# Which engine multiplies which scan state: eight transposed states in every scan order

## The chip, the cores and the metric

The kernel runs on one core of a Trainium2 chip. The metric is the device time of one execution in microseconds; all numbers are float32. Five engines work in it, each with its own queue that it follows in order: TensorE (PE: matmuls, transposes), VectorE (DVE: scans, products), ScalarE (ACT: activations, PSUM copies), GpSimd (POOL: products in SBUF) and SyncE (SP: the DMAs). They wait for each other with semaphores.

## The reference, cut to what matters

Eight images of 192 x 48 x 48 go through two layers. The first is a state-space layer: group norm, a projection to 384 channels, a 3x3 depthwise convolution and gelu give `u`, which is scanned in four orders (`k`: by rows, by columns, and both backwards).

```python
xs = jnp.stack([x_hw, x_wh, x_hw[..., ::-1], x_wh[..., ::-1]], axis=1)
def step(h, xs_t):                          # 2304 positions, 16 states for each of 384 channels
    d_t, u_t, B_t, C_t = xs_t
    dA = jnp.exp(d_t[..., None] * A)
    h = h * dA + (d_t * u_t)[..., None] * B_t[:, :, None, :]
    y = jnp.einsum('bkdn,bkn->bkd', h, C_t)  # sum over the 16 states
    return (h, y)
ys = ys[:, 0:2] + ys[:, 2:4, :, ::-1]
y = ys[:, 0] + ys[:, 1].reshape(Bb, Dd, Ww, Hh).transpose(0, 1, 3, 2).reshape(Bb, Dd, L)
```

`delta` (`d_t`) is the softplus of a small projection of `u`. After the scan come a layer norm over channels, a gate and an output projection; the second layer is an attention. The change touches the scan alone.

## The kernel before

**Chunks, orders, states.** One image's scan runs through four orders `k` of six chunks `c` of 384 positions each (24 chunks, numbered `q`), with 16 states `i` a chunk and three groups `j` of 128 channels a state. The loop over the eight images is a loop on the chip; the chunks are written out.

**What a state costs each engine.** ScalarE makes `dA` as exp into PSUM bank 2 + j (L1554), when the scan of the state before has read that bank. GpSimd makes delta times u times B for all three groups in one product (`delta_u_b`, L1794), three states ahead of the scan. VectorE scans (L1229), three instructions a state, into one of `NH = 4` state buffers `hb`. The last column of each state is saved by ScalarE as the start of the next chunk (`hold_state`, L1498, semaphore `carry`), because the product with C overwrites the buffer. Then the state is multiplied by its row of C and summed over the states into PSUM banks 5 to 7 (y), in one of three ways, which `Plan` fixes:

- *pool*: GpSimd multiplies by a broadcast row of C (`times_c`, L1804), after the scan and after `hold_state` of that state, and TensorE adds the result with an identity matmul (`state_sum`, L756, six passes).
- *dve*: ScalarE copies the row of C to PSUM bank 1 (`c_copy`, L1514), VectorE multiplies (`times_c`, L1257), and TensorE adds as above.
- *turn*: TensorE transposes the state in three tiles of 128 positions into PSUM bank 0 (`turn`, L734); ScalarE multiplies each tile by a column of C, as its per-partition scale, into one of three buffers `ht` (`turned_product`, L1523); TensorE transposes it back with a matmul that adds to y (`turned_sum`, L743). Bank 0 holds one tile, so the next can be turned only when ScalarE has read the last.

**The order on the queues.** TensorE goes through slots m = 0 to 15 of a chunk (slots 16 and 17 lie in the next chunk). In slot m it does delta's matmul (m = 1, 4, 7, for the next chunk), a *unit* if there is one, and then `slot(q, m)`: the sums that are due, and the tiles n + 1 + t = m of the turned states n, one or two. A dve state is summed in slot n + 2, a pool state in n + 3. In slots 5, 8 and 11 it adds a third of the y of the earlier orders (`y_chunk`, L820; L817 in order 0). ScalarE goes through steps i: for each j an exp, and after the second and third the products of the tiles of slot i - 1; then `hold_state(i - 1)`, a unit's copy (`unit_out`), the softplus's ln, `c_copy(i - 1)`, in steps 2 and 3 the stores of the last chunk's y (`store_y`, L1542), and the other softplus steps (abs, exp) of the next chunk's delta. VectorE does the scans of state i, then the product with C of state i - 1 if it is a dve state, and in steps 5, 8 and 11 delta (L1178). GpSimd does `delta_u_b(i + 3)`, then `times_c(i)` if i is a pool state, and after state 12 the next chunk's delta times u (L1779).

**PSUM bank 1** serves in turn delta's matmuls, the ln of the softplus, the rows of C, and the *units*: in orders 0 to 2 each chunk makes two 128-channel pieces of the next image's input projection (L787), whose copies (L1531, L1534) DMAs take away.

**The plans.** Orders 0 and 1 have four pool states (0, 3, 6, 9), five turned (1, 4, 7, 10, 13) and seven dve; orders 2 and 3 have three (0, 6, 9), seven (1, 3, 4, 7, 10, 12, 13) and six (2, 5, 8, 11, 14, 15). In the latter the slots 4 to 6 and 13 to 15 have two tiles.

**y by columns.** y lies in SBUF by rows. In orders 1 and 3 a chunk is eight columns; its 384 values are read and stored with a stride of 48 in SBUF, in the sequence in which PSUM holds them.

Of the kernel before, what the change touches and what calls it, by code (L numbers as in the profile page):

```python
# [97 lines left out]
LAST = PLANS[-1]  # L98

# [17 lines left out]
def made_s(b, q, n):  # L117
    return b * S_ALL + (LAST.ns + S_TO[q] + n)
# [36 lines left out]
UK = 3  # L155
# [9 lines left out]
def build(nc, t, out):  # L165
    ctx = ExitStack()
    with ctx:
# [465 lines left out]
        def _(e):  # L633
# [87 lines left out]
            def scan_phase(b, x_proj, turn_c):  # L721
# [43 lines left out]
                def slot(q, m):  # L765

                    p = plan(q)
                    for i in p.order:
                        if p.sum_at[i] == m and i in p.pool:
                            state_sum(q, i)  # L770
                    for at in p.slots[m][:1]:
                        tile(q, at)
                    if m == N + 1:
                        turned_sum(q, p.nt - 1)
                    for i in p.order:
                        if p.sum_at[i] == m and i in p.dve:
# [12 lines left out]

                def body(k, c, par, last, nxt):  # L790
                    g = e.snap(b * 24 + (c + k * NC))
                    q = k * NC + c
                    h = e.snap(b * UC + (c + k * NC)) if k < UK else None
                    for m in range(N):
# [7 lines left out]
                        if k < UK and m in plan(q).units:  # L802
                            unit(k, h, q, plan(q).units.index(m))
# [10 lines left out]
                        if m in ADD_AT:  # L814
                            j = ADD_AT[m]
                            if k == 0:
                                e.matmul(ps[:, 5 + j, 0:CH], d_diag[:, j], u_v[:, 0, j, ds(pos(k, c), CH)],  # L817
                                         start=False, stop=False)
                            else:
                                e.matmul(y_psum(k)[:, j], ident[:], y_chunk(k, c)[:, j], start=False, stop=False)  # L820
# [596 lines left out]
        def _(e):  # L1417
# [76 lines left out]
            def scan_phase(b):  # L1494
                def hold_state(k, c, i):
# [4 lines left out]
                def c_copy(g, q0, i, nxt, h=None):  # L1500
# [7 lines left out]
                    if nxt and i in (5, 8, 11):  # L1508
                        e.wait_ge(dp_v, g * 3 + (3 + (i - 2) // 3))
# [3 lines left out]
                    e.wait_ge(hcs, made_d(b, q0, d))  # L1513
                    e.activation(ps[:, 1, 0:CH], row_c[:, q % 2, i % ROWS], ACT.Copy).then_inc(c_ps, 1)  # L1514

                def turned_product(k, c, at):
# [4 lines left out]
                    e.wait_ge(turn_mm, made_t(b, q, at + 1))  # L1521
                    e.wait_ge(turn_sum, made_t(b, q, at - 2))
# [13 lines left out]
                def store_y(g, k, c, j, final=False):  # L1536
# [4 lines left out]
                    e.wait_ge(turn_sum, made_t(b, k * NC + c, plan(k * NC + c).nt))  # L1541
                    e.activation(y_chunk(k, c)[:, j], y_psum(k)[:, j], ACT.Copy).then_inc(yev, 1)  # L1542

                def body(k, c, par, last, nxt):
                    g = e.snap(b * 24 + (c + k * NC))
                    g16, g48, q = e.snap(g * 16), e.snap(g * 48), k * NC + c
                    h = e.snap(b * UC + (c + k * NC)) if k < UK else None
                    e.wait_ge(dp_v, g * 3 + 3)
                    for i in range(N):
# [378 lines left out]
```

## Time and profile before

| | |
|---|---|
| median of 3 runs | 14,696.73 us (14,694.96 to 14,697.96) |
| the profiled execution | 14,691.09 us, span 14,689.3 us |
| busy: TensorE, VectorE, ScalarE, GpSimd | 90%, 88%, 76%, 70% |
| granted TensorE clock | 0.991 |

The span is what lies between the first and the last instruction of the profiled execution. Busy shares are means over the scan and the other stages; the work of the scan repeats in 24 chunks an image and 192 in all, so 0.1 us a chunk is 19 us of the time.

### The profile page before, as it was taken

How to read it: one execution, taken by the hardware profiler on the slowest of the kernel's cores; microseconds unless marked ns; L12 is line 12 of the kernel's file. 1: busy time of each engine (PE TensorE's matmuls, PEld its weight loads, DVE VectorE, ACT ScalarE, POOL GpSimd, SP SyncE). 2: the span in 40 equal slices, each digit the busy share in tenths (PEclk: the TensorE clock that was granted, in tenths of full speed). 3: DMA queues.
4: the chain of work that ended last, by engine and by line, in shares of the span. 5: the costliest groups of instructions: out<-in, count | busy, mean ns of one | idle time of the engine just before them, and what ended most of it. 6: DMA issues, size and time to landing. Idle time of an engine off the chain costs nothing.

```text
span 14689.3 us, 247142 instructions
## 1 busy us (share of the span) xinstructions
PE 13181.2 (90%) x65256; PEld 8153.8 (56%) x65256; DVE 12970.4 (88%) x13833; ACT 11123.1 (76%) x22914; POOL 10326.6 (70%) x4126
## 2 busy tenths in 40 slices
PE   6888988889888998889988899888998889988899
PEld 4566455664556645566455664556645566455654
DVE  8999689996899978999689996899969999599995
ACT  5888578885788857887578876788767887678875
POOL 6999069980699807998079970899708996099960
PEclk9999999999999999999999999999999999999999
DMA  3443023430343303443033430344303442043420
GB/s 114 129 131 124 25 93 128 130 124 21 97 130 129 119 21 102 130 141 103 21 111 128 140 96 21 116 130 138 91 21 123 131 138 83 21 131 128 138 78 26
DMA packets 907982, 1468.60 MB, mean 100 GB/s; under 512 B 38912, under 2 KB 891904, under 8 KB 893664
## 3 DMA queue, kind: packets, MB, share of 16 engines
q1 hardware_dynamic: 906560, 1452.37, 31.2%
q8 instruction: 559, 9.16, 0.3%
q14 instruction: 863, 7.07, 0.1%
HBM read 1350.07 MB, written 102.17 MB: 99 GB/s over the span
## 4 chain that ended last, share of the span: by engine, by line
PE 33%; issue 24%; POOL 16%; DVE 15%; ACT 7%; DMA 2%; DVEq 1%; ACTq 1%; POOLq 0%; SPq 0%
POOL area L1794 12%; DVE area L1229 9%; PE ps L756 7%; PE ps L1030 5%; PE ps L1042 5%; DVE area L1257 4%; PE ps L743 3%; POOL area L1804 3%; PE ps L734 3%; ACT ps L1554 3%; DMA area<-bc_rows 2%; PE ps L892 2%; ACT area L1523 2%; PE ps L724 2%; PE ps L856 1%
## 5 line engine op out<-in xcount | busy, mean ns | idle before, releaser
L1229 DVE TENSOR_TENSOR_SCAN area<-ps,hst,area 128x384 f32<-128x384 f32 x9216 | 8581.8, 994 | 150.5 <-ACT ps L1554 69.6
L1794 POOL TENSOR_TENSOR area<-area 128x1152 f32<-128x1152 f32 x3072 | 7998.3, 2638 | 62.6 <-POOL area L1779 29.4
L1554 ACT ACTIVATE ps<-area,a_neg 128x384 f32<-128x384 f32 x9216 | 5259.7, 580 | 984.8 <-DVE area L1229 959.2
L756 PE MATMUL ps<-area,ident 128*128 128x384 f32 x11472 | 4127.3, 494 | 441.5 <-POOL area L1804 408.2
L756 PEld LDWEIGHTS ps<-area,ident 128*128 128x128 f32 x11472 | 2050.0, 191 | 1918.6 <-POOL area L1804 449.4
L743 PE MATMUL ps<-ident,area 128*128 128x128 f32 x20736 | 2882.2, 275 | 0.0
L743 PEld LDWEIGHTS ps<-ident,area 128*128 128x128 f32 x20736 | 2604.0, 192 | 50.3 <-ACT area L1523 1.5
L1523 ACT ACTIVATE area<-ps,area 128x384 f32<-128x384 f32 x3456 | 1972.6, 571 | 560.2 <-PE ps L734 559.4
L1714 ACT ACTIVATE area<-ps,t_neg,area 128x768 f32<-128x768 f32 x1728 | 1617.8, 986 | 1001.1 <-PE ps L1030 1001.1
L1774 POOL TENSOR_TENSOR area<-area,ones 128x2304 f32<-128x2304 f32 x16 | 85.2, 5352 | 3103.5 <-ACT area L1483 2980.9
L734 PE MATMUL ps<-ident,area 128*128 128x128 f32 x10368 | 1765.2, 279 | 326.4 <-ACT area L1523 314.0
L734 PEld LDWEIGHTS ps<-ident,area 128*128 128x128 f32 x10368 | 1260.7, 141 | 1334.1 <-ACT area L1523 568.9
L1804 POOL TENSOR_TENSOR area<-area 128x1152 f32<-128x1152 f32 x672 | 1771.5, 2636 | 153.0 <-DVE area L1229 123.5
L1257 DVE TENSOR_TENSOR area<-area,ps 128x1152 f32<-128x1152 f32 x1248 | 1658.7, 1329 | 17.0 <-ACT ps L1514 17.0
L1030 PE MATMUL ps<-area 64*128 64x384 f32 x6912 | 1374.7, 517 | 28.4 <-ACT area L1645 11.5
L1042 PE MATMUL ps<-area 128*64 128x384 f32 x6912 | 1322.8, 501 | 0.0
L1030 PEld LDWEIGHTS ps<-area 64*128 64x128 f32 x6912 | 604.2, 189 | 766.5 <-ACT area L1714 493.1
L1042 PEld LDWEIGHTS ps<-area 128*64 128x64 f32 x6912 | 441.7, 137 | 780.0 <-issue 776.9
L724 PE MATMUL ps<-area,w_dt 128*128 128x384 f32 (+1 forms) x1104 | 489.4, 525 | 360.7 <-DVE area L1257 356.7
L416 DVE SCALAR_TENSOR_TENSOR area<-area,w_dw 128x1152 f32<-128x1152 f32 (+1 forms) x640 | 802.7, 1329 | 0.0
L1514 ACT ACTIVATE ps<-area 128x384 f32<-128x384 f32 x1248 | 609.8, 489 | 93.7 <-DMA area<-bc_rows 70.2
L787 PE MATMUL ps<-xz,w_in 96*128 96x384 f32 x1152 | 445.5, 509 | 161.1 <-DVE area L1257 161.0
(163 smaller groups left out, 9539.6 us busy)
## 6 DMA issues: line engine op xcount, KB each, us to landing
area<-bc_rows SPq DMA_DIRECT2D x1536, 768.0 KB, 6.7
xz<-x_normed SPq DMA_DIRECT2D x144, 288.0 KB, 6.3
area<-in_x SPq DMA_DIRECT2D x18, 1728.0 KB, 10.1
area<-x_padded SPq DMA_DIRECT2D x24, 1250.0 KB, 12.1
z_raw<-z_st SPq DMA_DIRECT2D x144, 192.0 KB, 6.2
area<-z_raw SPq DMA_DIRECT2D x8, 3456.0 KB, 14.9
x_padded<-x_st SPq DMA_DIRECT2D x120, 200.0 KB, 7.8
x_normed<-area SPq DMA_DIRECT2D x9, 1728.0 KB, 8.1
```

What stands on the lines that cost most here:

```text
L734: i = e.matmul(ps[:, 0, j * 128:(j + 1) * 128], hb[:, n % NH, j, tt * 128:(tt + 1) * 128], ident[:], is_transpose=True)
L743: i = e.matmul(ps[:, 5 + j, tt * 128:(tt + 1) * 128], ht[:, at % 3, j * 128:(j + 1) * 128], ident[:], start=False, stop=False)
L756: m = e.matmul(ps[:, 5 + j, 0:CH], ident[:], hb[:, i % NH, j], start=i == 0, stop=i == N - 1)
L1030: i = e.matmul(ps[:, 2 * ((2 * m + h) % 3) + s, 0:CH], kz[rows, p, m * 128:(m + 1) * 128], q_v[rows, p, c * QC + s * CH:c * QC + (s + 1) * ...
L1042: i = e.matmul(ps[64 * h:64 * h + 64, 6 + s, 0:CH], vt[:, p, m, 64 * h:64 * h + 64], pb[:, w % 4, s * CH:(s + 1) * CH], start=m == 0, stop ...
L1229: e.tensor_tensor_scan(rev(hb[:, i % NH, j], k), rev(ps[:, 2 + j, 0:CH], k), rev(dbu[:, i % NH, j], k), hst[:, i, j:j + 1], ALU.mult, ALU. ...
L1257: e.tensor_tensor(hb[:, i % NH], hb[:, i % NH], ps[:, 1:2, 0:CH].broadcast_to([128, J, CH]), ALU.mult).then_inc(hcs, 1)
L1523: e.activation(ht[:, at % 3], ps[:, 0, 0:CH], ACT.Copy, scale=c_t[:, ds(t + (k % 2 * MT + tt), 1), k // 2 * N + n]).then_inc(turn_cp, 1)
L1554: e.activation(ps[:, 2 + j, 0:CH], dlt[:, par, j], ACT.Exp, scale=a_neg[:, j, k, i:i + 1]).then_inc(da, 1)
L1714: e.activation(pb[:, w % 4].rearrange("p (s l) -> p s l", s=2), ps[:, 2 * (w % 3):2 * (w % 3) + 2, 0:CH], ACT.Exp, scale=ksc[:, p, w:w + 1 ...
L1794: e.tensor_tensor(dbu[:, i % NH], du[:, par], row_b[:, q % 2, i % ROWS:i % ROWS + 1].broadcast_to([128, J, CH]), ALU.mult).then_inc(dbus, 1)
L1804: e.tensor_tensor(hb[:, i % NH], hb[:, i % NH], row_c[:, q % 2, i % ROWS:i % ROWS + 1].broadcast_to([128, J, CH]), ALU.mult).then_inc(hcp, 1)
```

## The change

All four orders get one plan: pool states 0, 9, 11; turned states 1, 3, 4, 6, 7, 10, 12, 13; dve states 2, 5, 8, 14, 15. Two tiles now lie in slots 4 to 9 and 13 to 15. State 11 is summed in slot 13. The units move to slots 12 and 14; the second one, and the adds of y, go ahead of the slot's second tile, and the sums of a slot with two tiles, those of pool states too, stand between the tiles. Bank 1's waits follow (`after_ln`, `ln_free`, unit 0 after the last delta, unit 1 after unit 0's copy). In orders 1 and 3 y is read and stored in runs of eight values in SBUF, and it is the PSUM side that goes with a stride of 48. Some sums of semaphore counts are worked out once a chunk.

```diff
 class Plan:
-    def __init__(self, pool, turn, units):
+    def __init__(self, pool, turn, units, early={}):
...
-        self.sum_at = {n: n + 3 for n in pool} | {n: n + 2 for n in self.dve}
+        self.sum_at = {n: n + 3 for n in pool} | {n: n + 2 for n in self.dve} | early
...
+        self.late = units[0] > 11
+        self.ln_free = max(n for n in self.dve if n < 10)
+        self.after_ln = {5: 1, 8: 2, min(n for n in self.dve if n > 10): 3}
...
-FIVE = Plan((0, 3, 6, 9), (1, 4, 7, 10, 13), (10, 14))
-SEVEN = Plan((0, 6, 9), (1, 3, 4, 7, 10, 12, 13), (10, 13))
-PLANS = (FIVE, FIVE, SEVEN, SEVEN)
+EIGHT = Plan((0, 9, 11), (1, 3, 4, 6, 7, 10, 12, 13), (12, 14), {11: 13})
+PLANS = (EIGHT,) * K
...
-            return y_v.rearrange("p j (h w) -> p j w h", h=H)[:, :, ds(c * 8 if k < 2 else (NC - 1) * 8 - c * 8, 8), :]
+            return y_v.rearrange("p j (h w) -> p j h w", h=H)[:, :, :, ds(c * 8 if k < 2 else (NC - 1) * 8 - c * 8, 8)]
...
-            return p if k % 2 == 0 else p.rearrange("p j (w h) -> p j w h", w=8)
+            return p if k % 2 == 0 else p.rearrange("p j (w h) -> p j h w", w=8)
...
-                def slot(q, m):
+                def slot(q, m, between=None):
 
                     p = plan(q)
-                    for i in p.order:
-                        if p.sum_at[i] == m and i in p.pool:
-                            state_sum(q, i)
+                    sums = [i for i in p.order if p.sum_at[i] == m]
+                    if len(p.slots[m]) < 2:
+                        for i in sums:
+                            if i in p.pool:
+                                state_sum(q, i)
                     for at in p.slots[m][:1]:
                         tile(q, at)
                     if m == N + 1:
                         turned_sum(q, p.nt - 1)
-                    for i in p.order:
-                        if p.sum_at[i] == m and i in p.dve:
+                    for i in sums:
+                        if i in p.dve or len(p.slots[m]) == 2:
                             state_sum(q, i)
+                    if between:
+                        between()
                     for at in p.slots[m][1:]:
                         tile(q, at)
...
                 def unit(k, h, q, i):
...
+                    if i == 1:
+                        e.wait_ge(unit_ev, h * 2 + 1)
+                    elif plan(q).late:
+                        e.wait_ge(dp_v, b * 72 + (3 * q + 6))
...
+                def filler(k, c, h, q, m):
+                    add_y(k, c, m)
+                    if k < UK and m == 14 and plan(q).late:
+                        unit(k, h, q, plan(q).units.index(m))
...
-                        slot(q, m)
+                        slot(q, m, lambda: filler(k, c, h, q, m))
...
-                    if nxt and i in (5, 8, 11):
-                        e.wait_ge(dp_v, g * 3 + (3 + (i - 2) // 3))
+                    if nxt and i in plan(q0).after_ln:
+                        e.wait_ge(dp_v, g * 3 + (3 + plan(q0).after_ln[i]))
...
-                            softplus(g + 1, 1 - par, nxt[0], "ln", LN_AT[i], h=h if i == 11 else None,
-                                     c8=made_d(b, q, plan(q).dve.index(8) + 1))
+                            softplus(g + 1, 1 - par, nxt[0], "ln", LN_AT[i], h=h if i == 11 and not plan(q).late else None,
+                                     c8=made[q] + (plan(q).dve.index(plan(q).ln_free) + 1))
```

## Rows read from the trace of the kernel before

**Rows 1.** The page's costliest groups; busy us and mean ns behind the bar.

```profile
L1794 POOL TENSOR_TENSOR area<-area 128x1152 f32<-128x1152 f32 x3072 | 7998.3, 2638 | 62.6 <-POOL area L1779 29.4
...
L1257 DVE TENSOR_TENSOR area<-area,ps 128x1152 f32<-128x1152 f32 x1248 | 1658.7, 1329 | 17.0 <-ACT ps L1514 17.0
```

**Rows 2.** Windows: one chunk of orders 0, 1, 2, 3; length, then busy us.

```profile
core 0: us, PE busy (x) PEld busy (x) DVE busy (x) ACT busy (x) POOL busy (x), PEclk, DMA share, GB/s
2139.15:2193.76 54.61, 45.78 (x223) 30.79 (x223) 54.27 (x60) 45.06 (x106) 54.37 (x21) 1.00 0.39 129
2466.91:2521.53 54.62, 47.34 (x222) 30.60 (x221) 54.02 (x60) 45.29 (x104) 54.38 (x21) 1.00 0.40 129
2791.24:2845.29 54.05, 48.15 (x264) 34.72 (x263) 52.97 (x58) 46.72 (x110) 51.92 (x20) 1.00 0.40 130
3060.65:3113.88 53.23, 47.75 (x255) 33.28 (x255) 52.89 (x58) 46.47 (x107) 51.94 (x20) 1.00 0.40 121
```

**Rows 3.** Timeline of GpSimd, order 2: start, us, instructions, idle before them.

```profile
2821.68 2.63 POOL L1804 TENSOR_TENSOR area<-area 128x1152 f32<-128x1152 f32 x1 [1.89 <-DVE area L1229]
...
2832.03 2.65 POOL L1804 TENSOR_TENSOR area<-area 128x1152 f32<-128x1152 f32 x1
...
2842.40 2.65 POOL L1779 TENSOR_TENSOR area<-area 128x1152 f32<-128x1152 f32 x1
2845.29 7.81 POOL L1794 TENSOR_TENSOR area<-area 128x1152 f32<-128x1152 f32 x3 [0.24 <-DVE area L1229]
```

**Rows 4.** Timelines of VectorE, order 2 and (last row) order 3.

```profile
2792.27 2.83 DVE L1229 TENSOR_TENSOR_SCAN area<-ps,hst,area 128x384 f32<-128x384 f32 x3 [1.01 <-ACT ps L1554]
...
2796.33 2.83 DVE L1229 TENSOR_TENSOR_SCAN area<-ps,hst,area 128x384 f32<-128x384 f32 x3
...
2819.76 5.73 DVE L1229 TENSOR_TENSOR_SCAN area<-ps,hst,area 128x384 f32<-128x384 f32 x6
...
3129.39 1.02 DVE L1229 TENSOR_TENSOR_SCAN area<-ps,hst,area 128x384 f32<-128x384 f32 x1 [0.26 <-ACT ps L1554]
```

**Rows 5.** Timeline of ScalarE, order 2, steps 5 to 9.

```profile
2814.11 0.58 ACT L1523 ACTIVATE area<-ps,area 128x384 f32<-128x384 f32 x1 [0.78 <-PE ps L734]
...
2815.09 1.08 ACT L1554 ACTIVATE ps<-area,a_neg 128x384 f32<-128x384 f32 x2
2816.11 0.57 ACT L1523 ACTIVATE area<-ps,area 128x384 f32<-128x384 f32 x1
...
2817.31 0.58 ACT L1523 ACTIVATE area<-ps,area 128x384 f32<-128x384 f32 x1 [0.16 <-PE ps L734]
...
2818.71 1.07 ACT L1554 ACTIVATE ps<-area,a_neg 128x384 f32<-128x384 f32 x2
...
2821.40 0.20 ACT L1498 ACTIVATE hst<-area 128x3 f32<-128x3 f32 x1
...
2823.85 0.58 ACT L1554 ACTIVATE ps<-area,a_neg 128x384 f32<-128x384 f32 x1
...
2824.87 1.08 ACT L1554 ACTIVATE ps<-area,a_neg 128x384 f32<-128x384 f32 x2
...
2827.77 1.08 ACT L1554 ACTIVATE ps<-area,a_neg 128x384 f32<-128x384 f32 x2
```

**Rows 6.** Timeline of TensorE, order 2: a tile, the sum of state 5, a tile, unit 1.

```profile
2816.73 0.55 PE L734 MATMUL ps<-ident,area 128*128 128x128 f32 x3 [0.77 <-ACT area L1523]
...
2823.04 2.10 PE L756 MATMUL ps<-area,ident 128*128 128x384 f32 x6
2824.97 0.49 PE L734 MATMUL ps<-ident,area 128*128 128x128 f32 x3
...
2839.88 1.56 PE L787 MATMUL ps<-xz,w_in 96*128 96x384 f32 x4 [0.75 <-DVE area L1257]
```

**Rows 7.** Groups of the y add in order 2, then add and store in order 3.

```profile
L820 PE MATMUL ps<-area,ident 128*128 128x384 f32 x36 | 14.6, 487 | 0.0
...
L820 PE MATMUL ps<-area,ident 128*128 128x384 f32 x24 | 17.4, 813 | 0.0
L1542 ACT ACTIVATE area<-ps 128x384 f32<-128x384 f32 x12 | 10.0, 831 | 0.5
```

More of the change, by code:

```diff
@@ L98 @@
 LAST = PLANS[-1]
+assert S_ALL % NC == 0 and all(not p.slots[N + 1] and max(map(len, p.slots.values())) < 3 for p in PLANS)
 def made_p(b, q, n):
@@ L117, in made_s @@
 def made_s(b, q, n):
-    return b * S_ALL + (LAST.ns + S_TO[q] + n)
+    return b * NC * (S_ALL // NC) + (LAST.ns + S_TO[q] + n)
 ADD_AT = {5: 0, 8: 1, 11: 2}
@@ L774, in slot, with add_y @@
                         turned_sum(q, p.nt - 1)
-                    for i in p.order:
-                        if p.sum_at[i] == m and i in p.dve:
+                    for i in sums:
+                        if i in p.dve or len(p.slots[m]) == 2:
                             state_sum(q, i)
+                    if between:
+                        between()
                     for at in p.slots[m][1:]:
                         tile(q, at)
+                def add_y(k, c, m):
+                    if m in ADD_AT:
+                        j = ADD_AT[m]
+                        if k == 0:
+                            e.matmul(ps[:, 5 + j, 0:CH], d_diag[:, j], u_v[:, 0, j, ds(pos(k, c), CH)],
+                                     start=False, stop=False)
+                        else:
+                            e.matmul(y_psum(k)[:, j], ident[:], y_chunk(k, c)[:, j], start=False, stop=False)
                 def unit(k, h, q, i):
                     e.wait_ge(hcs, made_d(b, q, plan(q).dve.index(plan(q).unit_after[i]) + 1))
+                    if i == 1:
+                        e.wait_ge(unit_ev, h * 2 + 1)
+                    elif plan(q).late:
+                        e.wait_ge(dp_v, b * 72 + (3 * q + 6))
                     e.wait_ge(xz_in, h * 16 + 16)
@@ L801, in body @@
                             delta_tile(*nxt, j, 1, 0 if last else 64)
-                        if k < UK and m in plan(q).units:
+                        if k < UK and m in plan(q).units and not (m == 14 and plan(q).late):
                             unit(k, h, q, plan(q).units.index(m))
@@ L810, in body @@
                             e.wait_ge(ct_cp, b * GM + GM)
-                        slot(q, m)
+                        slot(q, m, lambda: filler(k, c, h, q, m))
                         if m < 3 and m in LATE_X and not last:
                             x_proj(1, LATE_X[m])
[L814 to L820, printed above, removed]
                 walk(e, body)
@@ L1494, in scan_phase @@
             def scan_phase(b):
+                tiles, made = {}, {}
                 def hold_state(k, c, i):
@@ L1512, in c_copy @@
                     e.wait_ge(c_in[q % 2], g * 32 + (16 * (q // 2) + 16))
-                    e.wait_ge(hcs, made_d(b, q0, d))
+                    e.wait_ge(hcs, made[q0] + d)
                     e.activation(ps[:, 1, 0:CH], row_c[:, q % 2, i % ROWS], ACT.Copy).then_inc(c_ps, 1)
@@ L1520, in turned_product @@
                     t = c * 3 if k < 2 else (NC - 1) * 3 - c * 3
-                    e.wait_ge(turn_mm, made_t(b, q, at + 1))
-                    e.wait_ge(turn_sum, made_t(b, q, at - 2))
+                    e.wait_ge(turn_mm, tiles[q] + (at + 1))
+                    e.wait_ge(turn_sum, tiles[q] + (at - 2))
                     e.activation(ht[:, at % 3], ps[:, 0, 0:CH], ACT.Copy,
@@ L1540, in store_y @@
                         e.wait_ge(ysum, made_s(b, k * NC + c, plan(k * NC + c).ns))
-                    e.wait_ge(turn_sum, made_t(b, k * NC + c, plan(k * NC + c).nt))
+                    e.wait_ge(turn_sum, tiles[k * NC + c] + plan(k * NC + c).nt)
                     e.activation(y_chunk(k, c)[:, j], y_psum(k)[:, j], ACT.Copy).then_inc(yev, 1)
@@ L1547, in body @@
                     h = e.snap(b * UC + (c + k * NC)) if k < UK else None
+                    tiles[q], made[q] = e.snap(made_t(b, q, 0)), e.snap(made_d(b, q, 0))
                     e.wait_ge(dp_v, g * 3 + 3)
```

1 line of the change is left out of this document (removed).

## The prediction

> **What bounds the kernel now.** I read the page first, for which engines are nearly full and which lines fill them; then the windows, for one chunk of each scan order; then the timelines of GpSimd, VectorE, ScalarE and TensorE in one chunk of order 2, to see who waits for whom. The page shows two lines that carry the scan: GpSimd's products of 2638 ns, and VectorE's products with C of 1329 ns beside its scans [rows 1]. The windows split the scan by order [rows 2]. In orders 0 and 1 (five turned states, four on GpSimd) a chunk takes 54.61 and 54.62 us and GpSimd is busy for 54.37 of it: GpSimd sets the pace. In order 2 (seven turned, three on GpSimd) a chunk takes 54.05, in order 3 53.23; there GpSimd has some 2 us left over and VectorE is busy for 52.97 and 52.89. So one image's 24 chunks cost 6 x (54.61 + 54.62 + 54.05 + 53.23) = 1299 us, eight images 10,393 of the profiled 14,691.
>
> In order 2 I take the start of state 0's scan, 2796.33, as time zero [rows 4]; the next chunk's comes 54.03 later. Three things count. GpSimd waits 1.89 us before its product for state 6 and starts it at 25.35 [rows 3]. The row names a scan, but that state's scan was long done (7 and 8 run from 2819.76 [rows 4]); what came 0.28 earlier is ScalarE's copy of the scan's last column (hold_state), at 25.07 [rows 5], which must be saved before the product overwrites it. Then GpSimd runs without a gap to state 0 of the next chunk, starting at 48.96, ending at 51.6: 2.4 us before it is needed. ScalarE is the third: from slot 5 on it has no idle but its waits for TensorE's turned tiles, 0.78 and 0.16 us [rows 5]. Its exp for scan 8 is just in time: the six scans of states 7 and 8 take 5.73 [rows 4], and six at the pitch of the three in the row ahead (2.83) would take 5.57.
>
> **The change, part by part.** *Loads.* Orders 0 and 1 lose one GpSimd product: 54.62 - 2.59 (four products from 2821.68 to 2832.03 [rows 3]) = 52.03 us. Against order 3, VectorE loses one product with C: 53.23 - 0.26 (its wait [rows 4]) - 0.16 (the stretch above) - 1.25 (1.33 less overlap) = 51.6. By loads alone a chunk would take 52.0.
>
> *Where the work lands.* States 6 and 7 are now both turned, so slots 4 to 9 all have two tiles, where before only 4 to 6 had. A two-tile step on ScalarE with a C copy and one softplus step costs 3.62 (2815.09 to 2818.71); a one-tile step with the same costs 2.90 (2824.87 to 2827.77) [rows 5]. The second product can't start before TensorE has turned its tile after the first was read: 1.20 from product to product (2816.11 to 2817.31). So steps 8, 9 and 10 each grow by about 0.7.
>
> *A wait at slot 7.* There TensorE does delta, the first tile, the sum of state 5, and now a second tile, of state 6. That sum starts at 2823.04 and takes 1.93 [rows 6], so the tile is turned from 2824.97, at 28.64, and its product can start at 29.22 (0.58 from turn to product, 2816.73 to 2817.31). ScalarE is through with exp(8,2) at 28.0 (2823.85 plus 0.5). It waits 1.2, like the 0.78 that the same pattern costs at slot 4. Then product, hold and ln, 0.48 + 0.1 + 0.41 (2817.31 to 2818.71 holds a product, a hold and two operations like ln): exp(9) starts at 30.21, where it started at 28.54 before (2824.87). VectorE's delta and scan 9 come behind that ln, some 1.3 late: what the dropped product with C had given.
>
> *What is late next.* Step 9 costs 3.62: exp(10) at 33.83. In step 10 the hold comes after three exps and both products, 2.70 (2815.09 to 2817.31, and 0.48): state 9's last column is saved at 36.5. The product for state 9 on GpSimd waits for that, and starts 0.28 later at 36.8; before, state 9's product started at 35.7 (2832.03). Behind it now stand states 13, 14, the product for 11, 15, delta times u (2.89) and state 0 of the next chunk (2.64): 5 x 2.585 + 2.89 + 2.64 = 18.46. For the signal to VectorE I allow 0.3, as for the one above: 36.8 + 18.46 + 0.3 = **55.56** us, against 54.03. Moving GpSimd's state 6 to 11 puts one more product behind the latest wait in the chunk, and the new tiles make that wait later.
>
> *The chunk's end.* GpSimd's product for 11 ends at 47.2. TensorE, in slot 13, holds the second tile (state 12's first) behind its sum, so ScalarE's product of that tile comes at 49.9 and exp(15) ends at 51.0; scan 15 (three of 0.92) runs from 51.1 to 53.85. In order 3 the last product (state 13) comes at 52.7, the C copy for 14 ends at 53.7, VectorE's product ends at 55.2: hidden under 55.56. In orders 0 to 2 unit 1 (4 matmuls, 1.38; 1.56 in the row with its overlap [rows 6]) stands between the tiles of slot 14. The last product slips to 53.5, and unit_out, the C copy and VectorE's product follow: 0.48 + 0.1 + 0.4 + 0.45 + 1.3: **56.25**. The 1.01 us that VectorE waits at the end of order 2's chunks [rows 4] goes with the old unit 1 at slot 13; this is what takes its place.
>
> *y in runs of eight.* Adding y costs TensorE 813 ns a pass in order 3 against 487 in order 2, and storing it costs ScalarE 831 [rows 7]. Neither a run of eight in SBUF nor a stride of 48 in PSUM is in the trace. Best case: the row of order 2, 0.65 a pair less, and VectorE's 0.26 wait gone. Worst: as much again as now. The stores fall in steps 2 and 3, under slack; the add at slot 5 falls in a TensorE wait for ScalarE of some 0.9, so 0.65 hides and 1.3 shifts the chain by about 0.35. I take the row of order 2 and keep both ends. The Trainium skill (SBUF — State Buffer, Door 1: The DMA port swizzle) says that full bandwidth in SBUF needs accesses that stay within 16-byte lines, and that PSUM, with 8-byte lines, slows matmuls at any non-contiguous pattern; by it the change moves the cost from SBUF to PSUM and nothing is won, +0.35 x 12 chunks x 8 = 34 us. No row here shows such a matmul. The shorter semaphore arithmetic I cost at nothing: ScalarE's products start 0.5 behind the exp ahead of them, so no arithmetic shows there.
>
> **Sum.** 18 x 56.25 + 6 x 55.56 = 1346 per image, 47 more; times 8 = 375 us. The profiled execution took 14,691.1 (span 14,689.3), 5.6 under the median of three. Prediction 14,697 + 375 = 15,070.
>
> **The rivals.** *The loads decide* (faster). GpSimd at 52.03 gives 24 x 52.03 - 1299 = -50 per image, 14,295; if only the slot 7 wait holds, VectorE at 51.6 + 0.16 + 1.3 = 53.1 gives 14,490. For it: GpSimd never waits in orders 0 and 1, and the total load falls on both busiest engines. Against: GpSimd did wait 1.89 at state 6, and that chain had only 2.4 us of slack, of which the move takes 2.6. It decides if state 9's product can start before 35.4 (1299 / 24, the mean chunk now, less 18.76). The Trainium skill (Perfetto Trace Analysis, Identifying the Most-Contended Engine) tells to take the engine of highest occupancy and shorten it; by that rule the loads decide. Order 3's rows, where neither engine is full, bear the rule out only in part.
>
> *The chain is shorter than I think* (about the same). Without both TensorE waits (0.62 above a normal step at slot 4, 1.0 at slot 7) the GpSimd chain is 53.9 and the unit tail 54.6: 18 x 54.6 + 6 x 53.9 = 1306, +60; with the tail hidden too, 24 x 53.9, -40. So 14,655 to 14,755. Against: the wait at slot 4 is in the rows.
>
> *The PSUM stride costs more than the SBUF stride* (slower still): double the present penalty adds 1.0 in 12 chunks, 96 us: 15,130 to 15,200.
>
> *The y change does nothing*: it moves the forecast by 34 us at most and stays in its range.
>
> **How the numbers follow.** Main case 0.50; its range goes from the slot 7 wait hidden (1.0 less: 14,880) to the stride as dear as before and some more (15,130). Loads 0.25, shorter chain 0.17, stride 0.08. Leaving out the stride case and the lower half of the loads case, the range is 14,400 to 15,130. A measurement here can tell 0.2% (29 us) from no change. Faster: 0.25 plus 0.05 of the short chain, 0.30; within 0.2%: 0.08; slower: 0.50 + 0.08 + 0.04 = 0.62.
>
> **What would show it.** GpSimd idle 3 us or more before its product for state 9, starting 36 to 37 us after scan 0; VectorE's first scan of a chunk waiting for GpSimd in order 3 and for ScalarE in orders 0 to 2; ScalarE waiting a microsecond for a turned tile in step 8; exp and scan 9 behind it; chunks of 55.5 to 56.3 us. It is wrong if GpSimd has no gap and chunks take 52 to 53 us, and where state 9's product starts tells which step failed.

## The result and the profile after

The changed kernel takes 15,161.37 us (median of four runs, 15,155.23 to 15,163.03); the kernel before took 14,697.26 beside it. The ratio is 1.0314, with an interval of 1.0300 to 1.0329: 464 us slower, where 375 were forecast. The sign, the mechanism and its place came out as put; the time lies 31 us above the range of 14,400 to 15,130. The profiled execution has a span of 15,153.4, which is 464.1 more than that of before, so the profile shows the whole difference.

The page's costliest groups come first, to set against [rows 1]: busy us and mean ns behind the bar, then the idle time ahead of the group and what ended it.

```profile
L1246 DVE TENSOR_TENSOR_SCAN area<-ps,hst,area 128x384 f32<-128x384 f32 x9216 | 8599.8, 998 | 445.0 <-PE ps L759 194.1
L1814 POOL TENSOR_TENSOR area<-area 128x1152 f32<-128x1152 f32 x3072 | 7992.7, 2639 | 112.0 <-POOL area L1799 46.6
...
L1824 POOL TENSOR_TENSOR area<-area 128x1152 f32<-128x1152 f32 x576 | 1516.3, 2632 | 803.8 <-DVE area L1246 749.6
L1274 DVE TENSOR_TENSOR area<-area,ps 128x1152 f32<-128x1152 f32 x960 | 1290.4, 1344 | 218.1 <-ACT ps L1533 215.2
```

The work did fall: L1274, VectorE's products with C, has 960 instructions and 1290 us where it had 1248 and 1659. But GpSimd's products with C (L1824) now have 804 us of idle time ahead of them, and VectorE's have 218.

The windows say where. The first three are one chunk each of orders 0, 1 and 2, the next two are neighbouring chunks of order 3, and the last four are stretches of 3 us inside the second of these.

```profile
core 0: us, PE busy (x) PEld busy (x) DVE busy (x) ACT busy (x) POOL busy (x), PEclk, DMA share, GB/s
2148.04:2204.43 56.39, 49.76 (x286) 36.65 (x285) 52.11 (x57) 47.59 (x110) 51.83 (x20) 1.00 0.38 125
2486.43:2542.84 56.41, 49.78 (x286) 36.67 (x285) 52.11 (x57) 47.59 (x110) 51.84 (x21) 1.00 0.38 124
2824.88:2881.28 56.40, 49.76 (x286) 36.65 (x284) 52.09 (x57) 47.58 (x110) 51.90 (x21) 1.00 0.38 125
3108.43:3163.94 55.51, 47.68 (x278) 35.15 (x277) 52.05 (x57) 46.89 (x109) 51.93 (x21) 1.00 0.36 114
3163.94:3220.61 56.67, 49.08 (x278) 36.01 (x277) 52.29 (x57) 46.84 (x109) 51.89 (x20) 0.97 0.38 113
3172.94:3175.94 3.00, 1.92 (x8) 0.97 (x7) 3.00 (x4) 2.62 (x8) 3.00 (x2) 1.00 0.21 13
3175.94:3178.94 3.00, 1.94 (x4) 1.16 (x5) 3.00 (x4) 3.00 (x9) 3.00 (x2) 0.80 0.81 152
3178.94:3181.94 3.00, 3.00 (x13) 2.16 (x12) 2.76 (x4) 1.50 (x4) 3.00 (x2) 0.63 0.95 327
3181.94:3184.94 3.00, 3.00 (x16) 2.09 (x15) 3.00 (x4) 3.00 (x8) 3.00 (x3) 1.00 0.09 36
```

Beside [rows 2], in order 0 GpSimd went from 54.37 to 51.83 and VectorE from 54.27 to 52.11, near the loads that were worked out (52.03 and 51.6). The chunks went the other way, from 54.6 to 56.4. Now no engine is full: GpSimd idles some 4.5 us in each chunk of orders 0 to 2.

GpSimd's timeline answers [rows 3]. The first two rows are of an image's first chunk, the rest of one chunk in order 2, whose scan of state 0 starts at 2828.71.

```profile
2068.32 2.63 POOL L1814 TENSOR_TENSOR area<-area 128x1152 f32<-128x1152 f32 x1 [0.62 <-DVE area L1246]
2075.83 2.63 POOL L1824 TENSOR_TENSOR area<-area 128x1152 f32<-128x1152 f32 x1 [4.87 <-DVE area L1246]
...
2837.82 23.39 POOL L1814 TENSOR_TENSOR area<-area 128x1152 f32<-128x1152 f32 x9
2865.46 2.64 POOL L1824 TENSOR_TENSOR area<-area 128x1152 f32<-128x1152 f32 x1 [4.25 <-DVE area L1246]
...
2878.41 2.62 POOL L1799 TENSOR_TENSOR area<-area 128x1152 f32<-128x1152 f32 x1
2881.28 5.22 POOL L1814 TENSOR_TENSOR area<-area 128x1152 f32<-128x1152 f32 x2 [0.24 <-POOL area L1799]
```

But for 0.24 us behind delta times u, all the idle time of the chunk is one gap of 4.25 us ahead of the product for state 9, which starts at 36.75 (forecast 36.8). From there to delta times u (L1799) GpSimd never stops. The row names VectorE's scan, but ScalarE's timeline shows the copy of the last column 0.27 ahead of the product:

```profile
2857.90 0.58 ACT L1542 ACTIVATE area<-ps,area 128x384 f32<-128x384 f32 x1 [1.07 <-PE ps L737]
...
2858.89 1.08 ACT L1574 ACTIVATE ps<-area,a_neg 128x384 f32<-128x384 f32 x2
...
2865.19 0.20 ACT L1517 ACTIVATE hst<-area 128x3 f32<-128x3 f32 x1
...
2882.00 0.58 ACT L1542 ACTIVATE area<-ps,area 128x384 f32<-128x384 f32 x1 [0.88 <-PE ps L737]
...
2883.24 0.50 ACT L1533 ACTIVATE ps<-area 128x384 f32<-128x384 f32 x1 [0.19 <-ACT z_st L1553]
```

Against [rows 5]: ScalarE waits 1.07 in step 8 for a turned tile (forecast 1.2), starts exp(9) at 30.18 (30.21) and saves state 9's column at 36.48 (36.5). TensorE's timeline has the cause, the sum of state 5 and the tile behind it, turned from 28.66 on (28.64) as read off [rows 6]. It also has unit 1 (L807) at the chunk's end, and two sums of state 0 in order 3, one in each of the two chunks above.

```profile
2855.43 2.10 PE L759 MATMUL ps<-area,ident 128*128 128x384 f32 x6
2857.37 0.49 PE L737 MATMUL ps<-ident,area 128*128 128x128 f32 x3
...
2880.18 1.46 PE L807 MATMUL ps<-xz,w_in 96*128 96x384 f32 x4
2881.47 0.49 PE L737 MATMUL ps<-ident,area 128*128 128x128 f32 x3
...
3121.49 2.20 PE L759 MATMUL ps<-area,ident 128*128 128x384 f32 x6 [2.14 <-POOL area L1824]
...
3177.00 3.52 PE L759 MATMUL ps<-area,ident 128*128 128x384 f32 x6 [2.13 <-POOL area L1824]
```

VectorE's timeline in order 2, and in order 3 (last two rows), beside [rows 4]:

```profile
2858.99 0.56 DVE L1195 SCALAR_TENSOR_TENSOR area<-area,ps 128x384 f32<-128x384 f32 x1 [1.10 <-ACT ps L1488]
...
2873.50 5.56 DVE L1246 TENSOR_TENSOR_SCAN area<-ps,hst,area 128x384 f32<-128x384 f32 x6 [1.17 <-PE ps L759]
2879.67 2.83 DVE L1246 TENSOR_TENSOR_SCAN area<-ps,hst,area 128x384 f32<-128x384 f32 x3 [0.62 <-ACT ps L1574]
2883.86 1.35 DVE L1274 TENSOR_TENSOR area<-area,ps 128x1152 f32<-128x1152 f32 x1 [1.35 <-ACT ps L1533]
2885.13 1.01 DVE L1246 TENSOR_TENSOR_SCAN area<-ps,hst,area 128x384 f32<-128x384 f32 x1
...
3162.33 2.83 DVE L1246 TENSOR_TENSOR_SCAN area<-ps,hst,area 128x384 f32<-128x384 f32 x3 [1.88 <-ACT ps L1574]
...
3166.88 2.83 DVE L1246 TENSOR_TENSOR_SCAN area<-ps,hst,area 128x384 f32<-128x384 f32 x3 [0.41 <-POOL area L1814]
```

In order 2 the chunk's last wait is for ScalarE's copy of C (1.35, at 2883.86); GpSimd's product for the next chunk's state 0 (from 2881.28) is ready when that product with C ends. In order 3 VectorE's first scan waits 0.41 for GpSimd. Both chunk ends are those of the forecast. The wait of 1.17 at 2873.50 is one that it didn't have: scan 13 waits for TensorE's sum of state 9, whose buffer it takes, and that sum stands behind unit 0 in slot 12 (2869.98).

Last, y, to set against [rows 7]: the groups of the add and the store in order 3.

```profile
L795 PE MATMUL ps<-area,ident 128*128 128x384 f32 x24 | 9.7, 487 | 0.0
L1561 ACT ACTIVATE area<-ps 128x384 f32<-128x384 f32 x12 | 5.8, 486 | 0.6 <-PE ps L759 0.3
```

The add takes 487 ns instead of 813, the store 486 instead of 831: with runs of eight in SBUF and a stride of 48 in PSUM neither pays anything. The Trainium skill (SBUF — State Buffer, Door 1: The DMA port swizzle) says that non-contiguous PSUM patterns slow matmuls; this trace does not agree, at 487 ns for the strided write and for the contiguous one of before.

### The profile page after: what moved, and what is told of

The parts are those of the page before. It is cut to its first block, busy times and chain, and to the rows that moved or that the text cites. A ratio compares the mean times of both kernels' runs of the same rounds, so it can differ in the third digit from the quotient of the medians.

```text
span 15153.4 us, 265590 instructions
## 1 busy us (share of the span) xinstructions
PE 13627.7 (90%) x73320; PEld 8940.3 (59%) x73320; DVE 12713.2 (84%) x13545; ACT 11427.1 (75%) x23778; POOL 10080.9 (67%) x4030
## 4 chain that ended last, share of the span: by engine, by line
PE 37%; issue 27%; POOL 16%; DVE 10%; ACT 8%; ACTq 1%; DVEq 1%; POOLq 0%; DMA 0%; SPq 0%
POOL area L1814 11%; PE ps L759 8%; DVE area L1246 6%; PE ps L1047 5%; PE ps L1059 5%; PE ps L737 4%; POOL area L1824 4%; PE ps L746 4%; ACT ps L1574 3%; PE ps L727 2%; PE ps L909 2%; ACT area L1542 2%; DVE area L1274 2%; PE ps L873 1%; PE ps L807 1%
## 5 line engine op out<-in xcount | busy, mean ns | idle before, releaser
L1814 POOL TENSOR_TENSOR area<-area 128x1152 f32<-128x1152 f32 x3072 | 7992.7, 2639 | 112.0 <-POOL area L1799 46.6
L1574 ACT ACTIVATE ps<-area,a_neg 128x384 f32<-128x384 f32 x9216 | 5181.0, 577 | 428.8 <-DVE area L1246 409.6
L746 PE MATMUL ps<-ident,area 128*128 128x128 f32 x27648 | 3847.4, 275 | 0.0
L1542 ACT ACTIVATE area<-ps,area 128x384 f32<-128x384 f32 x4608 | 2639.9, 573 | 1311.6 <-PE ps L737 1311.4
L759 PE MATMUL ps<-area,ident 128*128 128x384 f32 x9168 | 3290.3, 495 | 372.8 <-POOL area L1824 281.4
L746 PEld LDWEIGHTS ps<-ident,area 128*128 128x128 f32 x27648 | 3472.5, 192 | 50.3 <-ACT area L1542 1.5
L737 PE MATMUL ps<-ident,area 128*128 128x128 f32 x13824 | 2424.6, 284 | 755.7 <-ACT area L1542 704.8
L737 PEld LDWEIGHTS ps<-ident,area 128*128 128x128 f32 x13824 | 1582.0, 141 | 2034.6 <-ACT area L1542 1432.6
L759 PEld LDWEIGHTS ps<-area,ident 128*128 128x128 f32 x9168 | 1650.7, 192 | 1330.1 <-POOL area L1824 439.3
L1824 POOL TENSOR_TENSOR area<-area 128x1152 f32<-128x1152 f32 x576 | 1516.3, 2632 | 803.8 <-DVE area L1246 749.6
L1274 DVE TENSOR_TENSOR area<-area,ps 128x1152 f32<-128x1152 f32 x960 | 1290.4, 1344 | 218.1 <-ACT ps L1533 215.2
L419 DVE SCALAR_TENSOR_TENSOR area<-area,w_cv 128x1152 f32<-128x1152 f32 x432 | 576.5, 1413 | 0.0
L1517 ACT ACTIVATE hst<-area 128x3 f32<-128x3 f32 x2560 | 507.7, 198 | 0.0
```

Source lines behind the costliest of these rows:

```text
L737: i = e.matmul(ps[:, 0, j * 128:(j + 1) * 128], hb[:, n % NH, j, tt * 128:(tt + 1) * 128], ident[:], is_transpose=True)
L746: i = e.matmul(ps[:, 5 + j, tt * 128:(tt + 1) * 128], ht[:, at % 3, j * 128:(j + 1) * 128], ident[:], start=False, stop=False)
L759: m = e.matmul(ps[:, 5 + j, 0:CH], ident[:], hb[:, i % NH, j], start=i == 0, stop=i == N - 1)
L1274: e.tensor_tensor(hb[:, i % NH], hb[:, i % NH], ps[:, 1:2, 0:CH].broadcast_to([128, J, CH]), ALU.mult).then_inc(hcs, 1)
L1542: e.activation(ht[:, at % 3], ps[:, 0, 0:CH], ACT.Copy, scale=c_t[:, ds(t + (k % 2 * MT + tt), 1), k // 2 * N + n]).then_inc(turn_cp, 1)
L1574: e.activation(ps[:, 2 + j, 0:CH], dlt[:, par, j], ACT.Exp, scale=a_neg[:, j, k, i:i + 1]).then_inc(da, 1)
```

## The experiments

The theory: the product for state 9 waits on GpSimd for state 9's column, six more operations stand behind it before the next chunk, and two-tile steps with the sum of state 5 make that column late; in orders 0 to 2 the chunk's end is set by unit 1, the last tile and the copy of C. The first rival: the second tile of each step, with TensorE's and ScalarE's hand-over, is the limit wherever GpSimd's products stand. The second: it is the y accesses. The chunk times below are the times from one GpSimd delta times u to the next.

**The product moved back to state 6.** The changed kernel, with GpSimd on 0, 6, 11 and state 9 turned in the place of 6.

```diff
-EIGHT = Plan((0, 9, 11), (1, 3, 4, 6, 7, 10, 12, 13), (12, 14), {11: 13})
+EIGHT = Plan((0, 6, 11), (1, 3, 4, 7, 9, 10, 12, 13), (12, 14), {11: 13})
```

> The changed kernel with GpSimd's middle state at 6 in place of 9 (9 is turned instead); every engine keeps the same number of operations of each kind. Loop theory (GpSimd's product for state 9 waits for ScalarE's hold of that state at 36.8 us, and seven GpSimd operations then stand between it and the next chunk's scan 0): the latest wait of a chunk is again the product for state 6, at about 25.4 us, and the product for 11 finds its hold done. GpSimd's free run of 52.0 then sets order 3, and the chunk's end (unit 1, C copy) sets orders 0 to 2 at about 52.4: 14,300 to 14,450 us, below the kernel before. Rival (24 turned tiles a chunk with their hand-over between TensorE and ScalarE are the limit, wherever GpSimd stands): chunks stay at 55.5 to 56.5, 15,100 to 15,200 us.

Measured: 14,735.55 (10 runs), ratio 1.0025 (1.0015 to 1.0035) to the kernel before, so 426 of the 464 us are gone with one state's place. The edit does two things at once, though: with state 9 turned in the place of 6, slot 7 holds one tile, and the wait there goes as well. What each is worth this run can't tell; the next two runs change one thing each. Chunks take 54.70 in orders 0 to 2 and 52.58 in order 3. GpSimd's timeline in order 1 shows two short gaps in place of the long one:

```profile
2397.74 2.63 POOL L1824 TENSOR_TENSOR area<-area 128x1152 f32<-128x1152 f32 x1 [2.34 <-DVE area L1246]
2400.32 13.02 POOL L1814 TENSOR_TENSOR area<-area 128x1152 f32<-128x1152 f32 x5
2413.54 2.63 POOL L1824 TENSOR_TENSOR area<-area 128x1152 f32<-128x1152 f32 x1 [0.20 <-ACT hst L1517]
```

VectorE's, at the end of the same chunk, shows why it isn't faster still: the exp is late by 0.91 and the copy of C by 1.35.

```profile
2421.64 2.83 DVE L1246 TENSOR_TENSOR_SCAN area<-ps,hst,area 128x384 f32<-128x384 f32 x3 [0.91 <-ACT ps L1574]
2425.82 1.35 DVE L1274 TENSOR_TENSOR area<-area,ps 128x1152 f32<-128x1152 f32 x1 [1.35 <-ACT ps L1533]
```

The rival of the tile hand-over falls: there are as many tiles as before, in as many two-tile slots. Order 3, where unit 1 runs nowhere, comes down to GpSimd's free run plus its gaps; orders 0 to 2 stop at the chunk's end, which the forecast of this run had priced too low (52.4), so that its time of 14,300 to 14,450 was missed.

**The column saved earlier.** The changed kernel, with the copy of the last column ahead of the second tile's product in ScalarE's steps.

```diff
+                                if j == 2:
+                                    hold_state(k, c, i - 1)
...
-                        if i >= 1:
+                        if i == 1:
```

> The changed kernel, with each hold of a state moved ahead of the second tile's product in its ScalarE step (it needs only the scan). Loop theory: in step 10 the hold comes earlier by that product and the wait for its tile, 0.16 + 0.48 + 0.1, so GpSimd's product for state 9 starts 0.7 earlier, at about 36.0 us after scan 0, and chunks get 0.7 shorter: 55.7 in orders 0 to 2, 54.8 in order 3, some 130 us less in all. Rival (the tile hand-over is the limit): the product moves by 0.7, the chunks don't, 0 us.

Measured: 14,931.29 (one run), 230 less; chunks 55.34 in orders 0 to 2 and 54.4 in most of order 3, GpSimd's gap at state 9 down from 4.25 to 3.18. That is more than was forecast (130 us, 0.7 a chunk): the product for state 9 starts at 35.65, 1.1 earlier, since exp(9) comes 0.3 earlier too (29.88). GpSimd's timeline in order 2:

```profile
2878.74 2.63 POOL L1826 TENSOR_TENSOR area<-area 128x1152 f32<-128x1152 f32 x1 [3.18 <-ACT hst L1517]
```

So the gap ends with the copy (L1517), which this row names as the releaser, and not with the scan that the row of the changed kernel named. And the chunks follow the product, which the rival of the hand-over denied.

**The sum of state 5 cut to a third.**

```diff
-                    for j in range(J):
+                    for j in range(2 if i == 5 else 0, J):
```

> The changed kernel with the sum of state 5 made for one channel group of three (two thirds of that state's part of y are left out), 1.3 us less of TensorE in slot 7, between the two tiles. If the wait of ScalarE in step 8 (1.07 us) is a link of the loop: it shrinks to about 0.15, the hold of state 9 and GpSimd's product for it come 0.9 earlier, and the chunks get about 0.9 shorter, 170 us in all. If the wait is covered by something else, the chunks stay within 0.2 us.

Measured: 14,969.59 (one run), 192 less; chunks 55.49, 0.91 less, and the wait in step 8 falls from 1.07 to 0.16. That sum between the two tiles of slot 7 is what makes exp(9), and with it the column of state 9, late.

**Half of unit 1.**

```diff
-                    for t in range(CT):
+                    for t in range(i, CT):
```

> The changed kernel with one of the two matmul halves of unit 1 (half of that projection's contraction is left out), 0.65 us less of TensorE between the tiles of slot 14. If the chunk's end sets orders 0 to 2 (unit 1, then state 13's product, unit_out, the C copy, VectorE's product), their chunks get 0.6 to 0.7 shorter, 55.7 to 55.8 from 56.40, and order 3 stays at 55.5: some 90 us in all. If GpSimd's queue sets them, they stay at 56.4.

Measured: 15,053.32 (one run), 108 less; orders 0 to 2 go from 56.40 to 55.75, order 3 stays at 55.5 and 56.7. So in orders 0 to 2 the loop runs on through unit 1 at the chunk's end, where half a unit is worth 0.65, and in order 3 it doesn't.

**The y accesses alone**, put into the kernel before (the views of y in SBUF and of its sum in PSUM).

```diff
-            return y_v.rearrange("p j (h w) -> p j w h", h=H)[:, :, ds(c * 8 if k < 2 else (NC - 1) * 8 - c * 8, 8), :]
+            return y_v.rearrange("p j (h w) -> p j h w", h=H)[:, :, :, ds(c * 8 if k < 2 else (NC - 1) * 8 - c * 8, 8)]
...
-            return p if k % 2 == 0 else p.rearrange("p j (w h) -> p j w h", w=8)
+            return p if k % 2 == 0 else p.rearrange("p j (w h) -> p j h w", w=8)
```

> The kernel before with nothing but the y access changed (runs of eight in SBUF, stride of 48 in PSUM, orders 1 and 3). If the PSUM stride is free, the y add falls from 813 to 487 ns a pass and the store from 831 to 487; order 3 loses VectorE's wait of 0.26 us a chunk, order 1 stays at GpSimd's 54.6: about 12 us less, too little to tell from no change by time. If a PSUM stride slows matmuls as the SBUF stride did, the add stays near 813 and the time does too; if it is dearer, order 3 grows by up to 1 us a chunk, 50 us.

Measured: 14,691.11, ratio 0.9996 (0.9986 to 1.0006). Order 3 falls from 53.23 to 52.86, orders 0 and 1 stay, and so does all of order 2 but its first chunk. The y accesses have no part in the loss.

**Keeping TensorE busy ahead of the sum of state 0 in order 3**, for the slow chunks there: first with three idle matmuls into bank 0.

```diff
+                        if i == 0 and q >= 3 * NC:
+                            e.wait_ge(turn_cp, made_t(b, q, plan(q).slots[3][0]))
+                            for _ in range(3):
+                                e.matmul(ps[:, 0, 0:CH], ident[:], w_dt[:, 0, 0:CH], start=True, stop=True)
```

> The changed kernel with three idle matmuls (their result in bank 0 is overwritten) ahead of state 0's sum in order 3, where TensorE waits 2.1 us for GpSimd. If the chunks of 56.7 in order 3 come from the granted clock that falls behind that wait, they go to 55.5 and none stays above 55.6, some 20 us in all; if they come from elsewhere, the mixture of 55.5 and 56.7 stays.

Measured: 15,260.89 (one run), order 3 at 57.3 to 59.0. Bank 0 made the idle matmuls wait for ScalarE, which TensorE's timeline shows (2.50 us of idle time ahead of them and of the sum):

```profile
3140.62 2.20 PE L756 MATMUL ps<-w_dt,ident 128*128 128x384 f32 x6 [2.50 <-ACT area L1546]
```

So the edit brought a wait of its own and settles nothing. The same into bank 1:

```diff
+                    if i == 0 and 3 * NC <= q < K * NC - 1:
+                        e.wait_ge(dp_rd, b * 72 + (3 * q + 4))
+                        for _ in range(3):
+                            m = e.matmul(ps[:, 1, 0:CH], ident[:], w_dt[:, 0, 0:CH], start=True, stop=True)
+                        m.then_inc(kept, 1)
...
+                        if q0 >= 3 * NC:
+                            e.wait_ge(kept, b * (NC - 1) + (q0 - 3 * NC + 1))
```

> The changed kernel with three idle matmuls into bank 1 (free there; ScalarE's C copy for state 2 waits for them) ahead of state 0's sum in order 3, so that TensorE's pause of 2.1 us for GpSimd is filled. If the chunks of 56.7 come from the granted clock that falls behind that pause, order 3 is 55.5 throughout; if not, the mixture of 55.5 and 56.7 stays.

Measured: 15,138.35 (one run), 23 less. Of the 32 chunk times of order 3 that the eight images give, 6 are 56.7 where 14 were; the slow chunk in order 2 (56.7 or 57.9) is untouched. The traces tell two kinds apart. In 11 of the 14 slow chunks of the changed kernel the sum of state 0 is stretched, to between 2.85 and 3.90 us from 2.20. Ahead of the other three it is the sum of state 11 at the end of the chunk before, 3.89 or 3.90 instead of 2.20 after a pause of some 1.6; in the 18 others both sums take 2.20. One such sum of state 11 in the changed kernel, and the windows on it:

```profile
5147.09 3.89 PE L759 MATMUL ps<-area,ident 128*128 128x384 f32 x6 [1.62 <-POOL area L1824]
```

```profile
5146.00:5149.00 3.00, 1.91 (x3) 1.07 (x4) 2.94 (x4) 0.90 (x2) 3.00 (x2) 0.70 0.00 0
5149.00:5152.00 3.00, 3.00 (x14) 1.88 (x12) 0.00 (x0) 0.66 (x3) 3.00 (x2) 0.73 0.36 87
```

With the idle matmuls (first row) no sum of state 0 in the 32 is stretched (second row), and all six slow chunks follow a stretched sum of state 11 (third row), whose pause the edit doesn't fill:

```profile
3120.91 2.10 PE L756 MATMUL ps<-w_dt,ident 128*128 128x384 f32 x6
3123.21 2.20 PE L765 MATMUL ps<-area,ident 128*128 128x384 f32 x6 [0.20 <-POOL area L1832]
...
7020.83 3.79 PE L765 MATMUL ps<-area,ident 128*128 128x384 f32 x6 [1.63 <-POOL area L1832]
```

So filling a pause took away every slow chunk behind that pause and left those behind the other. These are counts from one execution each, and they vary: the run with half of unit 1, whose order 3 is that of the changed kernel, has 16 of the first kind and 2 of the second.

**Toward a faster kernel.** State 6 on GpSimd with units at 10 and 12 instead of 12 and 14, then the same with the early copy:

```diff
-EIGHT = Plan((0, 9, 11), (1, 3, 4, 6, 7, 10, 12, 13), (12, 14), {11: 13})
+EIGHT = Plan((0, 6, 11), (1, 3, 4, 7, 9, 10, 12, 13), (10, 12), {11: 13})
...
+                        e.wait_ge(dp_v, b * 72 + (3 * q + 6))
```

> The changed kernel with GpSimd on 0, 6, 11 and the units in slots 10 and 12 (unit 1 then waits for the last delta as well). Loop theory: state 6's product waits 2.3 us for its hold, but three GpSimd operations fewer stand behind it, so only the chunk's end is above 52.6 in orders 0 to 2 (54.70 there, 52.58 in order 3 with units at 12 and 14); without unit 1 and its copy ahead of the C copy for 14 it loses 1.0 to 1.9 us: 52.8 to 53.7, and the time is 14,510 to 14,640, below the kernel before. Rival (TensorE's total is the limit, as the units are still there): 54.7 stays, 14,735.

> The same with each hold ahead of the second tile's product. The hold fills 0.1 of a wait for a tile in each two-tile step and takes 0.7 off the wait of GpSimd at state 6. If ScalarE's steps still bind somewhere in the chunk, 0.2 to 0.5 a chunk, 40 to 100 us; if GpSimd's free run of 52.0 binds, nothing.

Measured: 14,827.82, ratio 1.0093 (1.0076 to 1.0110), and with the early copy 14,739.77, ratio 1.0030 (1.0018 to 1.0041). Orders 0 to 2 take 55.27 and 54.78, where the first experiment had 54.70. The first misses its forecast of 52.8 to 53.7 and the rival's 54.7 too; the early copy takes off 0.49 and 88 us, as was expected of it. GpSimd's timeline shows the unit's price at its new place:

```profile
2370.21 2.62 POOL L1825 TENSOR_TENSOR area<-area 128x1152 f32<-128x1152 f32 x1 [2.17 <-ACT hst L1518]
```

This is the product for state 11, which waited 0.20 with the units late. ScalarE's timeline shows why: the unit stands ahead of the tiles of slot 10, and the second product there waits 1.57 us for its tile, where the first experiment has 0.16.

```profile
2365.72 0.58 ACT L1543 ACTIVATE area<-ps,area 128x384 f32<-128x384 f32 x1 [1.57 <-PE ps L737]
```

The column of 11 is late behind it: the same wait, one state on.

The early copy with units at 12 and 14:

> GpSimd on 0, 6, 11 with units at 12 and 14 (54.70 in orders 0 to 2, 52.58 in order 3) and each hold ahead of the second tile's product. Order 3 goes to 52.1, GpSimd's free run, as it did with units at 10 and 12; in orders 0 to 2 the hold fills a wait in the steps ahead of the C copy, 0.2 to 0.5 less: 54.2 to 54.5, and 14,600 to 14,680 us, just below the kernel before. If the chunk's end hangs on TensorE's tiles alone, 54.70 stays and the time is 14,700.

Measured: 14,665.52, ratio 0.9978 (0.9968 to 0.9988); 54.31 in orders 0 to 2, 52.15 in order 3, all as forecast. And seven turned states in all orders, GpSimd on 0, 6, 9, units at 10 and 13, without and with the early copy:

```diff
-PLANS = (EIGHT,) * K
+FIVE = Plan((0, 3, 6, 9), (1, 4, 7, 10, 13), (10, 14))
+SEVEN = Plan((0, 6, 9), (1, 3, 4, 7, 10, 12, 13), (10, 13))
+PLANS = (SEVEN,) * K
```

> The changed kernel's code with the old plan of orders 2 and 3 (GpSimd on 0, 6, 9; seven turned; units at 10 and 13) in all four orders. This is the step from four GpSimd states to three alone, without an eighth turned state. Loop theory: state 6's product waits for its hold, with 2.4 us to spare at the end, so chunks stay at the 54.03 of order 2 (order 3 at the 52.85 that the y access alone gave): 60 to 70 us below the kernel before. Rival (it is the fewer GpSimd states and the more tiles as such that cost): 55 or more in orders 0 and 1.

> The same with each hold ahead of the second tile's product. If ScalarE's two-tile steps bind at the end of the chunk (the 1.0 us wait of scan 15), 0.1 to 0.5 a chunk, 20 to 80 us more below the kernel before; in order 3, where VectorE is nearly full, 0.2 at most.

Measured: 14,680.48, ratio 0.9988 (0.9978 to 0.9997), and 14,611.06, ratio 0.9941 (0.9925 to 0.9958). The first has 54.20 in orders 0 to 2, against 54.03 in the forecast, and 52.86 in order 3; it is 18 us under the kernel before, where 60 to 70 were expected. The rival of this run (55 or more in orders 0 and 1) fails. The second is the fastest kernel here, 87 us under the kernel before by its ratio (0.0059 x 14,699); its chunks take 53.84 and 52.66. Its GpSimd still waits 1.73 once, at state 6:

```profile
2353.45 15.59 POOL L1818 TENSOR_TENSOR area<-area 128x1152 f32<-128x1152 f32 x6
2370.76 2.63 POOL L1828 TENSOR_TENSOR area<-area 128x1152 f32<-128x1152 f32 x1 [1.73 <-ACT hst L1519]
2373.34 7.82 POOL L1818 TENSOR_TENSOR area<-area 128x1152 f32<-128x1152 f32 x3
```

## Why the prediction was right in its mechanism, and wrong in its size

**The loads.** Right as loads, within 0.5 us (GpSimd 51.83 busy, forecast 52.03; VectorE 52.11, forecast 51.6), and right that they don't decide. The rival that they do fails at the point that the prediction named: state 9's product would have had to start before 35.4 and starts at 36.75. The Trainium skill (Perfetto Trace Analysis, Identifying the Most-Contended Engine) calls the engine of highest occupancy the most contended and would have it optimized first. In a chunk of order 0 the two fullest, GpSimd and VectorE, lost 2.54 and 2.16 us, and the chunk took 1.78 more, so this trace doesn't bear the rule out.

**The chain to state 9.** Right at each link, within 0.13 us (the wait in step 8, the tile, exp(9), the column, the product). The move put one more product behind the one for state 9, and that one starts 1.05 later than before (36.75 against 35.70). Cutting the sum of state 5, saving the column early and moving the product to state 6 each shortened the chunks of orders 0 to 2, by 0.91, 1.06 and 1.70 us: the first by what was forecast (0.9), the second by more (0.7), the third by less (4.0), since the chunk's end holds there. The rival that the chain is shorter fails with it. The rival of the dearer PSUM stride fails by the rows (487 ns), though its band of 15,130 to 15,200 is where the time came to lie: there the band was hit by accident. What y took off is too small for the run with y alone to tell (0.9996).

**The sizes.** Here the prediction failed. Its step "18 x 56.25 + 6 x 55.56" gave every chunk of an image the time of a regular one, and the upper end of the main case was made from the y term alone. Four terms of the sum were too small or missing, and together they carry the time over the range. The chunk times of the eight images give them.
- *The tail of orders 0 to 2*, put at 56.25, is 56.40. The last product comes at 53.29 (forecast 53.5) and the copy of C at 54.53 (54.48), but VectorE's product starts 0.62 after the copy's start, not 0.45. In the 16 regular chunks of orders 0 to 2 in each of eight images that is 19 us.
- *The order change.* The sum counted order 2's first chunk before at 54.05. It took 52.33, and now takes 56.40 like the others: 1.72 x 8 = 14 us.
- *Chunks slower than the rest.* The chain in order 3 was put at 55.56 and is 55.49 to 55.54 in 18 of the 32 chunk times, but 56.6 to 56.7 in 14, on average 56.02; one chunk of order 2 takes 56.7 in six images and 57.9 in two. (56.02 - 55.56) x 4 and (57.0 - 56.4) in eight images are 20 us. No term stood for it.
- *The first and the last chunk of an image.* The time from the last but one chunk of an image to the second of the next rose from 627.8 to 636.4 (means of seven), by 8.6, where the sum had 1.64 + 2.33; 8 x 4.6 is 37 us. Most is in the first chunk: from its first GpSimd product to its delta times u it took 55.53 in one image of before and 60.34 in one of after, 4.8 more, where the sum had 1.64. Before, GpSimd ran through this chunk but for one gap of 3.81; after, it has gaps of 2.44, 1.59, 1.43 and 0.62, and one of 4.87 ahead of state 9. VectorE waits 2.75 and 2.76 for TensorE's sum in both; after that it ran without a wait before, and now waits 0.88, 0.41, 1.10 and 1.17, the last two as in the regular chunk shown above. No experiment was made on this chunk, so its cause is read from the rows only.

These come to 90 us; 464 less 375 is 89.

**The slow chunks of order 3** come with a fall of the granted clock. After TensorE has paused 2.13 us for GpSimd's product of state 0, the sum takes 3.52 us instead of 2.20, and the two windows on it show 0.80 and 0.63 of full speed, which lie between the two levels of 2.4 and 1.2 GHz, so that each holds a part at either. The chunk is 1.16 longer. The second kind has the fall after a pause of some 1.6 us (windows of 0.70 and 0.73). Filling the first pause took away the first kind, 11 of 14, and left the second, so the pause is needed for the fall. It isn't enough: the chunk ahead has a pause of 2.14 and keeps its full clock. What decides between equal pauses is open, and so is what makes the one slow chunk of order 2 in each image.

## What to carry to other kernels

When work moves on an engine that runs its queue in order, look for the latest wait in the loop and count what stands behind it up to the next turn: here one product of 2.6 us was put behind the one for state 9, which came 1.05 us later as well, and a kernel in which two engines had less to do became slower by 3.1%. A copy that only releases a buffer deserves a place as early as its data allow: moving it by one instruction took 230 us from the changed kernel and 70 from the one with seven turned states. A sum over chunks should take the first chunk, the changes of order and the last chunk from rows of their own, since the regular ones had only 19 of the 89 us that were missing.

## What the hardware showed unexpectedly

A matmul of 128x384 in float32 that writes PSUM with a stride of 48 takes 487 ns, as the contiguous one does, and ScalarE's store from it 486; the same stride on the SBUF side cost 813 and 831 [rows 7]. And TensorE's granted clock fell inside a loop in which it is busy for 48 of 56 us, after pauses of 2.13 and of 1.62 us, in some chunks and not in others with the same pause; with the first pause filled, no fall came behind it.
